# Attention scores: from three bf16 parts on 96 rows to two fp32r parts on half arrays, with wider maxima and one ring of score banks

## The reference

```python
xd = (x @ W_down).reshape(b, t, h, s)              # 16 heads of 16 features
keys = jnp.einsum('bthk,hik->bthi', xd, tokeys) * scale
queries = jnp.einsum('bthk,hik->bthi', xd, toqueries) * scale
values = jnp.einsum('bthk,hik->bthi', xd, tovalues)
dot = jnp.einsum('bqhs,bkhs->bhqk', queries, keys)
attn = jax.nn.softmax(dot, axis=-1)
out = jnp.einsum('bhqk,bkhs->bqhs', attn, values).reshape(b, t, e)
return out @ W_unify + b_unify
```

## Time and profile before

| | us |
|---|---|
| median of 3 runs (lowest to highest) | 3145.11 (3143.08 to 3155.36) |
| the profiled execution's own time | 3149.36 |
| its span | 3147.6 |
| PE busy / DVE busy / ACT busy / POOL busy | 2916.1 / 2240.3 / 1850.9 / 745.7 |
| mean granted TensorE clock, share of full speed | 0.96 |

### The profile page before, as it was taken

The page is one execution under the profiler, slowest core; times in us unless marked ns, Lnnn a source line. Parts: engine busy times, 40 slices in busy tenths (PEclk is TensorE's granted clock), DMA queues, the critical chain, the costliest instruction groups (busy, mean ns, idle before and its releaser), DMA issues. The chain is left out here.

```text
span 3147.6 us, 57549 instructions
## 1 busy us (share of the span) xinstructions
PE 2916.1 (93%) x17263; PEld 1661.5 (53%) x17263; DVE 2240.3 (71%) x4484; ACT 1850.9 (59%) x3505; POOL 745.7 (24%) x759
## 2 busy tenths in 40 slices
PE   5999998859999999999999999999999859999987
PEld 3899998722333333333333333333333248999987
DVE  6655457548888887878887888888888376555565
ACT  5444456514666665766765666666666654444564
POOL 3353125440200300300200201101100034531353
PEclk8999999968999999999999999999999979999988
DMA  5211124231131231222212222231311052111242
GB/s 172 61 40 54 40 73 133 82 91 37 36 81 48 61 76 30 69 67 48 75 42 49 75 49 41 75 68 27 88 35 35 14 162 61 48 45 47 80 131 70
DMA packets 185826, 206.09 MB, mean 65 GB/s; under 512 B 29496, under 2 KB 149248, under 8 KB 185600
## 3 DMA queue, kind: packets, MB, share of 16 engines
q1 hardware_dynamic: 177408, 192.74, 22.7%
q0 software_dynamic: 8192, 10.57, 1.1%
HBM read 146.79 MB, written 55.66 MB: 64 GB/s over the span
## 5 line engine op out<-in xcount | busy, mean ns | idle before, releaser
L1486 DVE TENSOR_REDUCE at_mxc<-at_pb 128x1 f32<-128x512 f32 x2048 | 1297.1, 684 | 303.4 <-PE at_pb L1322 283.5
L1466 ACT ACTIVATE at_ex<-at_pd 128x512 f32<-128x512 f32 x2048 | 1099.6, 597 | 557.5 <-PE at_pd L1331 557.1
L1322 PE MATMUL at_pb<-at_ka,at_qa 96*128 96x512 bf16 x2048 | 802.0, 392 | 40.8 <-DMA at_qa<-at_scr 18.2
L1331 PE MATMUL at_pd<-at_qa,at_ka 99*128 99x512 bf16 x2048 | 779.9, 383 | 25.0 <-DMA at_qa<-at_mparts 19.7
L768 DVE TENSOR_TENSOR f_ml_hl<-f_ml_h,f_ml_hh 128x512 fp32r<-128x512 f32 (+1 forms) x384 | 288.1, 752 | 425.6 <-ACT f_ml_hh L844 424.6
L1322 PEld LDWEIGHTS at_pb<-at_ka,at_qa 96*128 96x128 bf16 x2048 | 200.2, 98 | 695.4 <-DVE at_mxc L1486 496.0
L1340 PE MATMUL at_po<-at_ex,at_va 128*32 128x512 f32 x4096 | 553.2, 610 | 9.6 <-DVE at_os L1574 5.6
L841 ACT ACTIVATE f_ml_h<-f_ml_pL,b1T 128x512 f32<-128x512 f32 (+1 forms) x384 | 244.1, 636 | 451.9 <-PE f_ml_pL L895 448.5
L910 PE MATMUL f_ml_pA<-f_wh,f_ml_hh 128*128 128x256 f32 (+1 forms) x1408 | 409.6, 291 | 0.0
L912 PE MATMUL f_ml_pA<-f_wl,f_ml_hh 128*128 128x256 f32 (+1 forms) x1408 | 402.1, 286 | 0.0
L913 PE MATMUL f_ml_pA<-f_wh,f_ml_hl 128*128 128x256 f32 (+1 forms) x1408 | 402.0, 286 | 0.0
(11 more groups left out here) (143 smaller groups left out, 2981.2 us busy)
## 6 DMA issues: line engine op xcount, KB each, us to landing
f_wraw<-in_L_ffn_w SPq DMA_DIRECT2D x128, 256.0 KB, 2.8
at_scr<-at_parts SPq DMA_DIRECT2D x96, 256.0 KB
at_ka<-at_scr SPq DMA_DIRECT2D x64, 256.0 KB, 5.2
at_qa<-at_scr SPq DMA_DIRECT2D x64, 192.0 KB, 3.9
f_ro_xr<-in_L_attn_x SPq DMA_DIRECT2D x16, 512.0 KB, 3.9
f_ml_xr<-in_L_attn_x SPq DMA_DIRECT2D x16, 512.0 KB, 4.2
x<-f_ml_yo SPq DMA_DIRECT2D x16, 512.0 KB, 4.0
at_xr<-x SPq DMA_DIRECT2D x16, 512.0 KB, 4.7
```

The costliest lines, as they stand in the source:

```text
L1322: eng.matmul(pb[place(c)][:, :], qa[g][0:KROWS, qh, j, qt * P:(qt + 1) * P], ka[g][0:KROWS, j, kh * 512:(kh + 1) * 512], start=True, stop= ...
L1331: eng.matmul(pd[place(c)][:, :], ka[g][0:KROWS + MROWS, j, kt * P:(kt + 1) * P], qa[g][0:KROWS + MROWS, qh, j, :], start=True, stop=True). ...
L1466: eng.activation(ex[t % 2][:, j, :], pd[place(GH * t + j)][:, :], ACT.Exp).then_inc(s_ex.sem, 1)
L1486: eng.tensor_reduce(mxc[:, c % CH:c % CH + 1], pb[place(c)][:, :], AX.X, ALU.max).then_inc(s_mx.sem, 1)
```

## The change

Queries and keys are held as two fp32r parts (high, low), and a score is a product over three slots: high x high, high x low, low x high. That is 48 rows, 50 with the maxima, which are two parts now. The heads of a group with even number lie on partitions 0 to 63, those with odd number on 64 to 127, so their products use the upper or lower half of the array's rows. `pb` becomes two tiles of two banks (1024 columns), one for each half; a maximum is taken over 1024 columns at once, and `negate` is gone. `px` is gone: the scores for the exponential *and* the side products go through one ring of three banks `pd`, in the order of PE's program; each bank has its own semaphore `s_free`, which is raised by whoever empties it. POOL has no parts to make. `times_v` stands behind the first pair. ACT copies `po`. The ones of `ka` are set at the start of attention by eight memsets of 32 partitions.

```diff
+Q_SLOTS = [0, 0, 1]
+K_SLOTS = [0, 1, 0]
+KROWS = len(Q_SLOTS) * HS
+MROWS = 2
+HALF = P // 2
+RING = 3
...
+class Ring:
+    def take(self):
+        self.n += 1
+        return self.n - 1
+    def full(self, n):
+        return n + 1 + self.per * self.i
+    def before(self, n):
+        return n // RING + self.per // RING * self.i
+    def freed(self, n):
+        return n // RING + 1 + self.per // RING * self.i
...
-        parts = sb("parts", [P, 2, 3, DT, T], BF16)
-        qa = [sb(f"qa{g}", [P, 2, GH, NQ], BF16) for g in range(4)]
-        ka = [sb(f"ka{g}", [P, GH, T], BF16) for g in range(4)]
+        parts = sb("parts", [P, 2, 2, DT, T], F32R)
+        qa = [sb(f"qa{g}", [P, 2, 2, NQ], F32R) for g in range(4)]
+        ka = [sb(f"ka{g}", [P, 2, T], F32R) for g in range(4)]
...
-        pb = [ps(f"pb{i}", [P, 512]) for i in range(BANKS)]
-        pd = [ps(f"pd{i}", [P, 512]) for i in range(BANKS)]
+        pb = [ps(f"pb{i}", [P, T]) for i in range(2)]
+        pd = [ps(f"pd{i}", [P, 512]) for i in range(RING)]
         po = ps("po", [P, 512])
-        px = ps("px", [P, 512])
+        ORDER = (1, 3, 0, 2)
...
+            def for_max(b, g, t, e, kh):
+                qh, p, qt = t // NT, t % NT // 4, t % 4
...
+                if kh == 0:
+                    eng.wait_ge(s_mx.sem, s_mx.at(2 * (ST * unit(b, g) + t) + e - 1))
+                rows = slice(HALF * e, HALF * e + KROWS)
+                mm = eng.matmul(pb[e][:, kh * NQ:(kh + 1) * NQ], qa[g][rows, qh, p, qt * P:(qt + 1) * P],
+                                ka[g][rows, p, kh * NQ:(kh + 1) * NQ], start=True, stop=True)
+                if kh == 1:
+                    mm.then_inc(s_b.sem, 1)
+
+            def for_exp(ring, b, g, t, j, n):
+                qh, kt, e, p = t // NT, t % NT, j % 2, j // 2
...
+                eng.wait_ge(s_free[n % RING].sem, s_free[n % RING].at(ring.before(n)))
+                rows = slice(HALF * e, HALF * e + KROWS + MROWS)
+                eng.matmul(pd[n % RING][:, :], ka[g][rows, p, kt * P:(kt + 1) * P], qa[g][rows, qh, p, :],
+                           start=True, stop=True).then_inc(s_full.sem, 1)
+            def side_product(ring, a):
+                bank = pd[a.n % RING]
+                eng.wait_ge(s_free[a.n % RING].sem, s_free[a.n % RING].at(ring.before(a.n)))
+                if a.after is not None:
+                    eng.wait_ge(s_free[a.after % RING].sem, s_free[a.after % RING].at(ring.freed(a.after)))
...
                     for i in range(4):
                         if ahead:
-                            scores_for_max(b1, g1, 4 * t + i)
-                        if not ends:
-                            scores(*((b, g, t + 1) if t < ST - 1 else (b1, g1, 0)), i)
-                        if i == 1:
-                            times_v(b, par, g, t)
-                    if now:
-                        aux(now)
+                            for_max(b1, g1, t, i // 2, i % 2)
+                        if tiles:
+                            for_exp(self.ring, *coming, ORDER[i], tiles[i])
+                        if i == 0:
+                            times_v(self.ring, b, par, g, t, done)
+                    if a:
+                        side_product(self.ring, a)
...
@@ ScalarE's step
+                    for i in range(4):
+                        if tiles:
+                            exponentials(self.ring, t + 1, ORDER[i], tiles[i])
+                        if i == 2 and t % NT == NT - 1:
+                            values_out(b, g, t)
+                    if a:
+                        side_out(self.ring, a)
...
@@ VectorE's step
+                    for e in range(2):
                         if ahead:
-                            maxima(b1, g1, 4 * t + i)
-                        if i == 1:
-                            aux(before)
+                            maximum(b1, g1, t, e)
+                        if e == 0 and self.late:
+                            side_out(self.ring, self.late)
+                    self.late = a
...
@@ GpSimd's start
+            for i, t in enumerate(ka):
+                for e in range(2):
+                    if i or e:
+                        eng.wait_ge(s_row, 2 * i + e)
+                    eng.memset(t[HALF * e + 32:HALF * (e + 1), :, :].bitcast(F32), 1.0).then_inc(s_row, 1)
+            class Do:
+                def before(self, sides):
+                    eng.wait_ge(s_row, 8)
+                    for f in range(2):
+                        norm.pow_step(eng, f, 4)
```

More of the change, by code:

```diff
@@ L1218, in phase @@
-                    do.step(b, par, g, t, n, ns, before, now, last)
-                    before = now
-        def place(c):
-            return 1 if c == ST * GH - 1 else c % BANKS
-        def back(c):
-            return next(d for d in range(1, ST * GH) if place((c - d) % (ST * GH)) == place(c))
-        unit = lambda b, g: 4 * b + g
-        next_unit = lambda b, g: (b, g + 1) if g < 3 else (b + 1, 0)
+                        a = self.place(task, b, par, g)
+                    do.step(b, par, g, t, coming, tiles, done, a, side, not ends, last)
@@ L1335, in times_v @@
+            def times_v(ring, b, par, g, t, done):
                 kt = t % NT
@@ L1418, in _, with end @@
+                def end(self, sides):
+                    for a in sides:
+                        side_product(self.ring, a)
             Walk(eng, Do())
```

452 lines of the change are left out of this document (214 added, 238 removed).

## The result

| | before | after |
|---|---|---|
| median of the runs (lowest to highest), us | 3149.99 (3143.08 to 3155.36, 4 runs) | 3968.41 (3949.04 to 3972.81, 4 runs) |
| the profiled execution's own time, us | 3149.36 | 3971.09 |
| mean granted TensorE clock | 0.96 | 0.83 |

The ratio is 1.259, 95% interval 1.2535 to 1.264: 26% slower. The forecast was 3577 us with a range of 3480 to 3730; its direction holds, its size does not, and the time lies outside the range.

The account below looks back on a forecast made before the run. Waits in the loops through ACT and DVE, not PE's work, were taken to set the step: loop and DMA waits 2192 against 1766 us (+426), start +6, giving 3577 us, range 3480 to 3730.

Parts of the forecast that it names:

- maximum over 1024 columns: DVE's maximum in the score loop: 1.20 us alone, bounds 1.10 and 1.37, against 0.684 for 512 columns.
- plain step: Attention step without a side task: 3.30 us instead of 2.85, set by DVE's loop; bounds on the increase +0.25 and +0.60.
- step behind f, qk, u / behind mx, no large product of its own: Step after a side task DVE empties: held ring bank delays the third pair, adding 1.94 us, for mx 1.53.
- a large product in the step: Side product on PE waits for its ring bank: u or xd +1.1 us, qk or v +0.2.
- copy of `po` in the step: ACT copies `po` ahead of the fourth exponential after steps 7 and 15: +0.4 us in 8 steps a batch.
- the term for the clock: TensorE's clock in the attention loop: the forecast's sum added nothing for a slower clock.
- rival 1: Clock falls because PE idles in held steps: one step in six at 1.2 GHz, +110 us, about 3690; chance 0.24.
- The DMA term: Waits for the maxima's DMA in unit g = 2 of seven batches: 21 us, as before; bounds -20 and +60.
- The start: Start of attention: POOL's memsets delay the norm's power by 8.7 us, the first unit's maxima save 2.6; together +6.
- Halves that do not work side by side: Score pairs on the array's two halves cost 0.46 us each: +50 us, about 3630; chance 0.11.
- A held bank that costs nothing: Ring bank held by DVE's emptying adds no time: the holds' 375 us go, about 3200; chance 0.08.
- Faster: Second pair starts while the values' products still run, result at 0.5 not 1.5: loop 1336, about 2720 us; chance 0.05.

Follow-up runs that it names:

- the run that empties first: The changed kernel with one edit, the order on DVE: the side task's bank is emptied ahead of the step's first maximum, not behind it; 3338.6 us, ratio 1.058.

## Why the prediction was wrong

**What held, at the level it was made for.** The reading that the loops decide and not PE's work, and each loop's size:

| | forecast | measured at 2.4 GHz |
|---|---|---|
| second pair behind the values' products | 1.00 | 1.00 |
| maximum over 1024 columns | 1.20 | 1.22 |
| plain step | 3.30 | 3.24 to 3.32 |
| step behind f, qk, u / behind mx, no large product of its own | 5.24 / 4.83 | 5.07 to 5.11 / 4.67 |
| a large product in the step: qk or v / u or xd | +0.2 / +1.1 | +0.4 to 0.5 / +1.3 |
| copy of `po` in the step | +0.4 | +0.43 to 0.5 |
| products of a pair | side by side | 0.00 to 0.01 apart |

The run with the full-array filler is the changed kernel near the full clock. Its medians over the 64 places of the six middle batches, at that level, add up to some 282 us (two places that are hardly ever at it filled in with their like). 2.8 of them are the filler behind "mx" and 2.8 the wait for the maxima: 276 without these, forecast 277. That it is so close is in part luck: held steps came out 0.15 shorter than forecast, steps with a large product 0.2 longer. One sum in the working does not come out, either: 2.74 and 0.05 give 2.79 and not 2.88 for the next first pair, with which DVE's loop is 3.21 and ACT's, at 3.23, decides. Measured are 3.24 at the least.

For the whole loop I took each step's time at the full clock from this kernel and from the runs with fillers (without the filler's own time): some 2167 us, where the forecast had 2192. Of the difference 19 are the DMA's waits, below. The run with the full-array filler has 95 more than 2167: 59 for its 44 slow steps, 6 for steps slow in part, 22 for the filler and some 8 in other steps, the DMA's waits among them.

**What failed: the term for the clock.** The forecast put it at nothing, and rival 1, "the clock falls" (0.24), at 110: "if one step in six runs at 1.2 GHz and costs 1.3 us more". It was 182 steps, not 85. Against the same places at the full clock they cost some 305 us, 1.7 each, and 99 more steps that are at the lower level for a part of their length some 90: together some 395, not 110. Both factors were short. The number, because I counted slow steps one by one, as accidents of a wait: they lie in 92 stretches, 57 of them one step long but nine of them four to twelve steps (of the sixteen of the unit from which the last two timelines after the result are, nine are slow). The price, because a loop that passes through PE's products three times is stretched in each: the second pair starts 0.87 later behind the values' products, the pair behind it 0.25 later again (1668.63 to 1669.23 against 1503.14 to 1503.49), and the next step's first pair 0.30 further ahead of the values' products.

The cause is shown from two sides. The filler of full-array products changes nothing but what PE does in the gaps behind the held bank, and takes 300 net off the loop. The order on DVE takes the gaps themselves away and the slow steps fall to 10%. So the gaps behind the held bank bring the clock down. How much comes back also depends on what fills them: six half-array products fill them too, and gave 154 of the loop (2408.7).

The reason I gave against it, "in the loop the clock is 0.99 now with short waits in every step", was a number of the kernel before, whose PE was busy for 390 of the 400 us of that row, 98%. The forecast had idle times of 1.9 us in it and did not ask what share of the loop they are: 28 x 1.9 of 277 us, 19%, to which its own plain step adds, with 2.0 us of PE's work in 3.30. In the window of the changed kernel PE idles 20%, slow steps included; in its steps wholly at the full clock it is 24%.

The Trainium skill, TensorE: Matmul & The Clock Gate, Part 1, says that the gate goes by how busy PE has lately been, and in its section "A second HAM failure mode: psum-queue depth-cycling" that frequent small idle times make it swing between its levels. The second is what the changed kernel shows, at 80% busy and a clock of 0.79. By the first alone the run with all products on one half, 93% busy at 0.54, should not be slow; there the measurement decides.

**The DMA term**, "as before", 21 us, was 19 too high in the changed kernel, which waits 2 us there, and only because its steps are slow. With short steps the same transfers cost 74 us, and the other order of the stores gave 76 back. I had put its bounds at -20 and +60; they were asked of the wrong kernel.

**The start**, "+6", was +24. POOL's part is as said, a little more:

```profile
639.13 14.78 POOL L1641 MEMSET at_ka<- 32x2048 f32 x8
654.00 1.04 POOL L165 TENSOR_TENSOR at_ln_rstd<-at_ln_ve,neghalf 128x4 f32<-128x4 f32 x1
```

The power stands at 654.00 where it stood at 643.00, +11 against +8.7. The other 13 us were left out: ahead of the loop the side products now go through the ring, each behind the emptying of the one ahead, and at 1.2 GHz:

```profile
695.66 2.04 PE L1390 MATMUL at_pd<-at_bd,at_xn 128*128 128x128 f32 x8 [0.90 <-ACT at_va L1483]
...
705.10 2.05 PE L1385 MATMUL at_pd<-at_xn,at_bd 128*128 128x512 f32 x2 [1.50 <-DVE at_parts L1557]
```

The same products, x8 and x2, took 1.1 us each in the kernel before. How the 24 us grow can be read from the first store and from the first product for the maxima, before and after:

```profile
671.50 6.44 SPq L1251 DMA_DIRECT2D at_scr<-at_parts  x6
...
692.98 19.94 PE L1322 MATMUL at_pb<-at_ka,at_qa 96*128 96x512 bf16 x34 [18.22 <-DMA at_qa<-at_scr]
```

```profile
689.71 5.81 SPq L1253 DMA_DIRECT2D at_scr<-at_parts  x4
...
716.52 1.22 PE L1343 MATMUL at_pb<-at_ka,at_qa 48*128 48x512 f32 x4 [2.27 <-DMA at_qa<-at_scr]
```

The store comes 18.2 later, 7.2 more than the power: that much lies in the side products and the making of the parts. The first product for the maxima comes 23.5 later: 5.3 are the larger stores and the loads. From there to the values' products it is 42.4 before and 43.1 after, so the 2.6 forecast as a gain of the long maxima are not to be seen. No run changed the order of the ring there, so the share of the ring against that of the clock in the 7.2 stays open.

**The other rivals.** Halves that do not work side by side (0.11): excluded by the starts. A held bank that costs nothing (0.08): excluded by 314 us of waits and by the run that empties first. Faster (0.05): the second pair starts 1.00 behind the values' products, as now.

**The balance.** In the profiled executions 3971.1 - 3581 = 390 us are to be found: some 395 of the clock, less the 25 by which the loop at the full clock is under 2192, 18 at the start, 2 behind the loop and in rounding. In terms of the edit: the place of the values' products costs 134 us by itself in the kernel before; taking it back in the changed kernel gives 645, taking back the order on DVE 630, both together 795. The two do not add, since either alone already takes most of the slow steps away (36% to 8 and 10%).

## What to carry to other kernels

When a change shortens PE's work but not the loop that it stands in, write down PE's new idle times and price every product in the loop at 1.2 GHz before setting the range: here 20% idle went with some 395 us on top of some 2167. The idle share is a warning and not a measure of the clock: 15% idle without the long gaps went with 0.95, 9% idle with half-array products in the gaps with 0.86. In a ring of shared banks, whoever empties a bank last sets the step, so the emptying goes ahead of the long instruction and the products that feed the slow engine ahead of those that wait for it. And a transfer that is hidden today is hidden by the length of today's steps: ask again once they are short, and look at what stands ahead of it in the program that issues it.

## What the runs showed of the hardware

- The granted clock does not follow PE's busy time alone. 93% busy with fp32r products on 48 rows, one after the other, gave 0.54; 92% busy with bf16 products on 96 rows gave 1.00, and 97% busy with fp32r products on 48 and 50 rows, in pairs on both halves, 0.99. With equal busy time (1447 to 1450 of 1600 us) the filler alone moved the clock: six fp32r products on 48 rows 0.86, two fp32 products on 48 rows 0.96, two on 128 rows 0.98.
- Products of two heads on the two halves of the rows, in different banks, start 0.00 to 0.01 us apart where neither waits, at both levels of the clock; pairs follow each other 0.23 apart at 2.4 GHz and 0.42 at 1.2. The first pair behind the values' products or behind a wait is 0.33 to 0.35 ahead of the next.
- A maximum over 1024 columns of PSUM, across two banks, takes 1.22 us, against 0.68 for 512; back to back their starts are 1.14 apart.
